# Cross-attention with a gated mix and an eight-expert feed-forward on one core: masks filled earlier, one h on ScalarE, two weight chunks loaded later

## The reference

```
h      = (x - mean(x)) / sqrt(var(x) + 1e-5)                 # layernorm over the 256 columns
normed = h * rsqrt(mean(h*h) + 1e-6) * norm_w
pool   = concat([normed, ctx], positions)                    # 256 keys
logits = (normed @ q_w.T) @ (pool @ k_w.T).T / 16            # causal for the first 128 keys
h_t    = softmax(logits) @ pool
alpha  = sigmoid(h @ gate_w.T + gate_b)
x2     = x + (1 - alpha) * h + alpha * h_t
xn     = layernorm(x2), as 2048 token rows
for each expert e of 8 (tok = top_idx[:, e], 512 rows):
    y   = gelu(xn[tok] @ W1[e] + b1[e]) @ W2[e] + b2[e]       # 256 -> 1024 -> 256, tanh gelu
    acc[tok] += y * combine_weights[tok, e]
out    = x2 + acc                                            # acc starts at zero
```

## Time and profile before

| | us |
|---|---|
| median of three runs | 276.34 (276.28 to 276.38) |
| profiled execution | 277.63 |
| its span, first to last instruction | 275.8 |
| TensorE busy | 265.7 (96% of the span) |
| VectorE / ScalarE / GpSimd busy | 219.0 / 188.2 / 155.9 |
| mean granted TensorE clock | 0.991 |
| chain that ended last | TensorE 83%, VectorE 6%, waiting for issue 4%, GpSimd 3%, ScalarE 2%, DMA 1% |

### The profile page before, as it was taken

One profiled execution on the slowest core, in us unless ns is written; L12 is line 12 of the kernel. 1 busy time (PEld: TensorE's weight loads), 2 busy tenths in 40 slices (PEclk: granted clock), 3 DMA queues, 4 the chain that ended last, 5 costly groups with the idle time before them and its releaser, 6 DMA issues.

```text
span 275.8 us, 5127 instructions
## 1 busy us (share of the span) xinstructions
PE 265.7 (96%) x1474; PEld 226.7 (82%) x1474; DVE 219.0 (79%) x554; ACT 188.2 (68%) x349; POOL 155.9 (57%) x153
## 2 busy tenths in 40 slices
PE   6999999999989999999999999999999999999992
PEld 2688899999866888888888888888888888888992
DVE  1788999898986499968878896796887889689452
ACT  2488898887575976685677587658657758763540
POOL 4283865655843956556446466655645646605515
PEclk9799999999999999999999999999999999999998
DMA  7993247568454956455565544546555461201211
GB/s 219 358 263 94 77 123 218 155 214 276 114 182 123 350 160 157 124 192 167 138 195 163 154 139 135 157 122 209 156 138 189 156 175 53 67 26 47 62 38 69
DMA packets 30292, 42.44 MB, mean 154 GB/s; under 512 B 5251, under 2 KB 24015, under 8 KB 30148
## 3 DMA queue, kind: packets, MB, share of 16 engines
q1 hardware_dynamic: 25392, 30.00, 34.4%
q0 software_dynamic: 4608, 12.24, 15.4%
q10 hardware_dynamic: 276, 0.00, 0.1%
HBM read 33.54 MB, written 9.24 MB: 155 GB/s over the span
## 4 chain that ended last, share of the span: by engine, by line
PE 83%; DVE 6%; issue 4%; POOL 3%; ACT 2%; DMA 1%; DVEq 0%; POOLq 0%; ACTq 0%
PE bank L1398 19%; PE bank L1185 13%; PE bank L1186 12%; PE bank L1187 12%; PE bank L1399 10%; PE bank L1229 4%; PE bank L1274 3%; PE bank L1326 2%; PE bank L1345 1%; PE bank L1349 1%; PE bank L1346 1%; DMA x_all<-in_x_dram 1%; PE bank L1181 1%; POOL out_dram L552 1%; PE bank L1258 1%
## 5 line engine op out<-in xcount | busy, mean ns | idle before, releaser
L742 ACT ACTIVATE keysT<-bank,biasT 128x512 f32<-128x512 f32 x63 | 43.7, 693 | 55.6 <-PE bank L1187 41.8
L552 POOL DMA_INDIRECT out_dram<-h,sidx x32 | 36.8, 1151 | 41.9 <-DVE h L1077 37.0
L543 POOL DMA_INDIRECT x_all<-out_dram,idx_all x32 | 35.4, 1106 | 23.9 <-DMA out_dram<-h,sidx 16.5
L1185 PE MATMUL bank<-x_hi,w_parts 128*128 128x512 f32 (+1 forms) x114 | 45.1, 396 | 0.0
L1186 PE MATMUL bank<-x_lo,w_parts 128*128 128x512 f32 (+1 forms) x114 | 44.4, 389 | 0.0
L1187 PE MATMUL bank<-x_hi,w_parts 128*128 128x512 f32 (+1 forms) x114 | 44.1, 387 | 0.0
L1102 DVE TENSOR_TENSOR g_lo<-keysT,g_hi 128x512 fp32r<-128x512 f32 x32 | 22.1, 690 | 24.9 <-ACT g_hi L743 23.4
L1398 PE MATMUL bank<-w_parts,g_hi 128*128 128x512 f32 x112 | 40.5, 396 | 0.0
L539 POOL DMA_INDIRECT x_all<-token_rows,idx_all x28 | 29.0, 1036 | 19.4 <-DVE factor L1126 7.7
L1107 DVE TENSOR_TENSOR w_parts<-w_raw,w_parts 128x512 fp32r<-128x512 f32 x56 | 38.9, 696 | 0.0
L748 ACT CAST w_parts<-w_raw 128x512 fp32r<-128x512 f32 x56 | 34.9, 623 | 0.0
(11 more groups left out here) (186 smaller groups left out, 685.9 us busy)
## 6 DMA issues: line engine op xcount, KB each, us to landing
w_raw<-in_L_ffn_W_dram SPq DMA_DIRECT2D x32, 512.0 KB
idx_rows<-in_L_ffn_top_idx_dram SPq DMA_DIRECT2D x8, 256.0 KB, 4.0
out_dram<-x SPq DMA_DIRECT2D x8, 256.0 KB, 3.0
hn_cnat<-in_ctx_dram SPq DMA_DIRECT2D x7, 256.0 KB, 2.7
token_rows<-xn SPq DMA_DIRECT2D x7, 256.0 KB, 2.2
hn_cnat<-in_L_ffn_b_dram SPq DMA_DIRECT2D x1, 1024.0 KB, 6.9
x_all<-in_x_dram SPq DMA_DIRECT2D x3, 256.0 KB, 4.4
x_all<-in_x_dram SPq DMA_DIRECT2D x1, 768.0 KB, 8.1
```

What stands on the lines that cost most here:

```text
L543: g.indirect_dma_start(accg[:, t, :], None, flat, list_of(e, t)).then_inc(acc_in[t], 16)
L552: g.indirect_dma_start(flat, idx(sidx[:, t:t + 1].bitcast(U32), 0), newrow[:, t, :], None, bounds_check=N - 1, oob_is_err=False).then_inc( ...
L742: a.activation(g32[:, f % NG, :], ps_up[f % 2][:, :], ACT.Gelu_apprx_tanh, bias=bias)
L1185: t_.matmul(dst, lhs_hi, rhs_hi, start=first, stop=False)
```

## The change

- Start: k_w is loaded by ScalarE's queue, ahead of norm_w, and not by SyncE's. norm_w and gate_b are loaded with one value per partition, and spread by four transposes of a broadcast column in place of the product with a row of ones. M's second half is made ahead of the first hn transposes, the context's transposes and copy ahead of the query. One more warm-up product. On VectorE both halves of M_lo come ahead of hnT_lo; the statistics of batch rows 6 to 9 are split and end behind pair 0's gate logits.
- Expert 0's chunks 2 and 3 are issued in rounds 0 and 1 of SyncE's loop over pairs, and expert 1's chunks 2 and 3 behind b2 after the loop. The last list part is loaded after the last rows' stores. ScalarE waits for chunk 2 in pairs 2 and 4, for chunk 3 in pair 6.
- Pairs 6 and 7: ScalarE makes h of pair 7, as a scaled and shifted identity. VectorE makes `stats2` and `aggr2` right behind the residual, and `shift` behind the gate logits. Piece 5 of expert 0's low weights goes from GpSimd to VectorE. GpSimd gathers tiles 0 and 1 in pair 7 ahead of rstd and tiles 2 and 3 behind it. ScalarE makes its weight piece earlier in pair 7 and later in pair 6.
- Passage: the products of late and early rows are put in another order; the first half of the last late_lo comes ahead of the last shift.
- Masks: `seen` is filled as 1024 float32 numbers whose bits are two bfloat16 ones, and masks are made before expert 1's gathers, when the last rows are ready.
- End: the last two up blocks come before the down products of blocks 4 to 7, which all go tile by tile; the waits before the last scatters stand in the scatters themselves.

The core of the diff (names of semaphores that follow from it, and repeated lines, are left out):

```diff
+    ONE_ONE = 1.0 + 0x3F80 / 2 ** 23
+        def stats_first(pair):
+            return isinstance(pair, int) and pair >= LAST - 1
...
@@ SyncE
-            load_weight(1, k_w, wts_in)
-            for c in range(NCH):
-                sp.dma_start(w_chunk_dst(c), w_chunk(0, c)).then_inc(w_in[c], 16)
+            for c in range(2):
+                load_chunk(0, c)
...
                 if r == LAST:
...
+                    sp.wait_ge(onehot_rdy, NB - EARLY)
+                    load_lists(IDX_PARTS - 1)
-                if r % 2 == 1:
+                if r < 2:
+                    load_chunk(0, 2 + r)
+                if r in (1, 3):
                     sp.wait_ge(wlo0_rdy, r + 1)
-                    sp.dma_start(w_chunk_dst(r // 2), w_chunk(1, r // 2)).then_inc(w_in[r // 2], 16)
+                    load_chunk(1, r // 2)
             sp.wait_ge(pv_mm, NPAIR)
             row_broadcast(b2_bc, b2.rearrange("e h -> (e h)")).then_inc(b2_in, 16)
+            for c in range(2, NCH):
+                sp.wait_ge(wlo0_rdy, 2 * c + 2)
+                load_chunk(1, c)
@@ GpSimd, attention
                 if is_last(p):
-                    gather_first_rows(range(1, NT))
+                    gather_first_rows(range(2))
...
-                    if not is_last(p):
+                    if not stats_first(p):
                         expert0_lo(p - 1)
                     rstd(p - 1, 1 - s)
-                if p == LAST - 1:
-                    gather_first_rows(range(1))
+                if is_last(p):
+                    gather_first_rows(range(2, NT))
@@ GpSimd, after the pairs
+            pool.wait_ge(pv_mm, NPAIR)
+            pool.wait_ge(last_xn[1], 1)
+            g.memset(seen_pairs, ONE_ONE).then_inc(consts, 1)
+            pool.wait_ge(consts, 4)
+            for t in range(NT):
+                g.affine_select(out=seen[:, t, :], ...).then_inc(seen_rdy, 1)
             for s in range(2):
                 pool.wait_ge(xn_out[s], ...)
                 pool.wait_ge(x2_out[s], ...)
             gather_rows(1, 1)
-            pool.wait_ge(pv_mm, NPAIR)
-            g.memset(seen, 1.0).then_inc(consts, 1)
...
@@ ScalarE
+            act.dma_start(wts[:, 1, :, :], k_w.rearrange("(k p) h -> p k h", p=P)).then_inc(wts_in, 16)
...
+            def last_h_rows():
+                act.wait_ge(hs_rdy, 5)
+                act.wait_ge(xh_rdy, LAST - 1)
+                act.wait_ge(diff_rdy, 2 * LAST - 2)
+                for b in range(2):
+                    a.activation(h[:, 1, b, :], x3[:, 2 * LAST + b, :], ACT.Identity, bias=last_h_shift[:, b:b + 1],
+                                 scale=pow_out[:, 0, 2 * LAST + b:2 * LAST + b + 1]).then_inc(h_rdy, 1)
...
+                if is_last_but_one(p):
+                    last_h_rows()
+                if is_last(p):
+                    expert0_hi(p)
...
-                    for c in range(NCH):
+                    for c in range(2):
                         act.wait_ge(w_in[c], 16)
+                elif not isinstance(p, int) and s == 0:
+                    act.wait_ge(w_in[2], 16)
+                if not is_last(p) and not is_last_but_one(p):
+                    expert0_hi(p)
@@ VectorE, attention
                     residual(p - 1, 1 - s, last_use)
+                    if stats_first(p):
+                        stats2(p - 1, 1 - s)
+                        aggr2(p - 1, 1 - s)
...
+                    if stats_first(p):
+                        shift(p - 1, 1 - s)
-                    if not is_last(p):
+                    if not stats_first(p):
                         h_rows(p + 1, 1 - s)
@@ VectorE, after the pairs (last_pair_low is the late_lo[2] of one row)
+            last_pair_low(0)
             last_pair_shift(1)
...
+            last_pair_low(1)
-            for piece in range(NPAIR - 2, NPAIR):
+            for piece in range(NPAIR - 3, NPAIR):
@@ TensorE, start
             M_rows(0)
+            M_rows(1)
             hn_transposes(0, 0)
-            M_rows(1)
-            t_.matmul(banks[7][:, :], ones_row[:, :], vec_rows[:, :], start=True, stop=True).then_inc(bc_mm, 1)
+            for n in range(2):
+                for k in range(KH):
+                    last = t_.transpose(banks[7][:, ...], norm_w_gate_bT[:, n, k:k + 1].broadcast_to([P, P]), ident[:, :])
@@ TensorE, last_downs and expert
-                    for f in range(NF - 3, NF):
+                    for f in range(NF - 4, NF):
-                    if not (is_last(e) and f == NF - 1):
+                    if not (is_last(e) and f >= NF - 2):
                         down(e, s, f - 2)
```

More of the change, by code:

```diff
@@ L147, in build_xattn_moe @@
             .rearrange("p (t c) -> p t c", t=NT)
+        seen_pairs = normed[:, :, :, :].rearrange("p s b h -> p (s b h)")
         cnat_last = x_all[:, NT * ROW:NT * ROW + 2 * H].rearrange("p (b h) -> p b h", b=2)
@@ L301, in each_pair, with is_last_but_one @@
             body(LAST, 1, 3)
+        def is_last_but_one(pair):
+            return isinstance(pair, int) and pair == LAST - 1
+        def stats_first(pair):
+            return isinstance(pair, int) and pair >= LAST - 1
         def has_second_next(pair):
@@ L949, in attention @@
                 if is_first(p):
+                    x_aggregates(6, 10)
+                    x_variances(6, 10)
                     h_rows(1, 1, False)
                     x_stats(10, NB, 4)
-                else:
+                elif not stats_first(p):
                     stats2(p - 1, 1 - s)
@@ L958, in attention @@
                 else:
-                    aggr2(p - 1, 1 - s)
-                    if not is_last(p):
+                    if stats_first(p):
+                        shift(p - 1, 1 - s)
+                    else:
+                        aggr2(p - 1, 1 - s)
+                    if not stats_first(p):
                         h_rows(p + 1, 1 - s)
@@ L971, in attention @@
                     dve.wait_ge(x_steps, steps[0])
-                elif not is_last(p):
+                elif not stats_first(p):
                     shift(p - 1, 1 - s)
@@ L1017, in _ @@
             last_pair_mixed(0)
-            shift(NPAIR - 2, 1 - last_s)
             last_pair_variance(0)
@@ L1030, in _ @@
                             ALU.mult, ALU.add).then_inc(last_xn[1], 1)
-            for b in range(2):
-                dve.wait_ge(late_hi_rdy, 3 + b)
-                dve.wait_ge(last_xn[b], 1)
-                v.tensor_tensor(late_lo[2][:, b, :], xn_last[:, b, :], late_hi[2][:, b, :].bitcast(F32),
-                                ALU.subtract).then_inc(late_lo_rdy, 1)
+            last_pair_low(1)
             def x_lo_part(e, s):
@@ L1250, in attention @@
                         .then_inc(setup_mm, 1)
-                    pe.wait_ge(log_rdy, 2 * NPAIR - 1)
-                    pe.wait_ge(late_hi_rdy, 1)
-                    for b in range(2):
-                        late_rows(0, b, late_hi, first=b == 0)
                 pe.wait_ge(exp_rdy, 2 * p + 2)
@@ L1264, in attention @@
                 if is_last(p):
-                    early_rows(range(1))
+                    pe.wait_ge(log_rdy, 2 * NPAIR - 1)
+                    pe.wait_ge(late_hi_rdy, 1)
+                    for b in range(2):
+                        late_rows(0, b, late_hi, first=b == 0)
                 pe.wait_ge(pT_ev, p + 1)
```

111 lines of the change are left out of this document (64 added, 47 removed).

## The result

The changed kernel took 280.57 us (median of four runs, 279.08 to 281.75) against 276.31 before: a ratio of 1.0151 (95% interval 1.0101 to 1.0201). The forecast was 273.8, faster. The profiled execution took 280.89, its span is 279.1.

A forecast was written before the change was run, and what follows sets the result against it. Nothing starves TensorE in the expert stage, so slack lies in the start, passage and end. Terms 1.6 - 0.7 + 1.0 + 0.65 = 2.55 us off the median 276.34 gave 273.8 us, range 272.0 to 276.0.

The forecast's parts named there:

- The weight chunks: Late loads of expert 0: ScalarE waits 1.4 us for chunk 2 in pair 2; cost 0.7 us, from 0 to 1.2.
- The start: Up to pair 2's logits: earlier query starts pair 0's logits at 12.35, gain 1.6 us at pair 2, from 0.3 to 2.6.
- Rival 1: Start: clock stays at half through the first query, costing 1.3 us, total 275.1; chance 0.17.
- The passage: Pairs 6 and 7 to the first x_hi, set by VectorE: gain 1.0 us, from 0.4 to 1.4.
- The masks: Masks ahead of expert 1's gathers end at 86.5 to 87.4 and cost nothing, with 1.3 us in hand.
- rival 3: Masks hold VectorE: three weight pieces each behind a select make g_lo(0) 2.3 us late, total 275.3; chance 0.07.
- rival 4: Last list load, moved behind the last rows, holds ScalarE before expert 0's second gelu: 4 us lost, 277.8; chance 0.06.
- The expert stage: Expert products on TensorE: nothing starves them and they stay in place, so the stage can only begin earlier.
- The end: Last up product before block 4's down products: first scatter 0.8 us earlier, gain 0.65, from 0.3 to 0.9.

The follow-up runs named there:

- e5: Kernel before, unchanged, profiled again in a single execution: 276.01 us.
- e1: Changed kernel with all four chunks of expert 0 loaded at the start again, as before: 275.79 us, ratio 0.9975 to before.
- e3: Changed kernel with chunk 2 loaded at the start and only chunk 3 late, in round 1: 277.44 us, ratio 1.0037 to before.
- e9: e1 with the new 8-byte tensor of ScalarE's h declared behind all others: 275.04 us, ratio 0.9944 to before.
- e12: e1 with a pad declared between the weights and x_hi: 276.25 us, ratio 0.9989 to before.
- e15: Kernel before with ten warm-up products, not nine: 276.21 us, ratio 0.9980 to before.
- e11: Changed kernel with one late chunk a round, ScalarE's wait for chunk 2 in pair 4 only, and the new 8-byte tensor declared last: 275.07 us, ratio 0.9948.
- e10: Kernel before with one unused 8-byte tensor declared at the place of the new one: 277.17 us, ratio 1.0029 to before.
- e8: e1 with the end of the kernel before: 276.58 us, ratio 0.9999 to before.
- e13: e11 with the last list loaded where it was before, ahead of the last store of x2: 274.65 us, ratio 0.9931 to before.
- e14: Kernel before with only chunks 2 and 3 of expert 0 loaded late, in rounds 0 and 1: 281.81 us, ratio 1.0190.
- e7: Kernel before, unchanged, profiled once more in a single execution: 277.74 us.

## Why the prediction was wrong

The profiled execution after against e5, an ordinary execution of before, by stretches of TensorE's timeline and chain:

| stretch | before (e5) | after | change | forecast |
|---|---|---|---|---|
| to the logits of pair 2 | 30.28 | 29.69 | -0.6 | -1.6 |
| to those of pair 4 | 15.44 | 17.15 | +1.7 | +0.7 |
| to those of pair 5 | 7.72 | 11.70 | +4.0 | 0 |
| to those of pair 7 | 14.84 | 14.84 | 0 | 0 |
| to the first product of expert 0 | 15.69 | 14.93 | -0.8 | -1.0 |
| to expert 1's transposes | 11.72 | 12.06 | +0.3 | 0 |
| to the last transposes | 135.89 | 136.55 | +0.7 | 0 |
| to the end of the span | 42.62 | 42.18 | -0.4 | -0.65 |
| span | 274.2 | 279.1 | +4.9 | -2.55 |

- **The weight chunks** are the step that failed: costed at 0.7, they took 4.8 us by e1, 5.7 in the profiled execution. The forecast followed chunk 2 to the wait of ScalarE, and there its mechanism was right and only the size off: the load left at 33.70, behind the list as foreseen, ScalarE stood 2.1 and not 1.4, and 1.5 to 1.7 of it reached TensorE. The term that was too small is the landing: the cast behind the wait starts at 39.55, some 5.8 us after the issue, against 5.0. (Halfway between 4.1 and 6.9 would have been 5.5; the sum took a third.) For chunk 3 it asked when the chunk is wanted ("in pair 6 only") and not what is queued behind it: in round 1 it goes out with expert 1's chunk 0, and the context of pair 5 comes next. That is 1.65 by itself (e3), 4.0 in the profiled execution, where the clock falls behind the wait.
- **The start** was near by its own steps (12.35, with two errors that cancel; at pair 2 a gain of 2.2 on the trace, forecast at 1.6) and wrong in the base. The forecast saw that the trace lay 1.3 above the median, and took the gain off the median all the same. But those 1.3 were the half clock at 8 to 11 us, which the change removes and an ordinary execution does not have: against e5 the start gains 0.6, and 0.0 to 0.5 with all chunks early (e9 30.26, e1 30.09, e12 29.74). Rival 1, the clock staying at half, did not come: the four spreading transposes take 0.62, near the 0.60 at full clock, and e15 shows that the tenth warm-up product alone is enough in the kernel before.
- **The passage** was right by the traces: 0.8 against 1.0, mix(6) at 0.69 as foreseen. No run undoes it alone.
- **The masks** cost nothing, as foreseen; rival 3 did not come. VectorE's three pieces took 2.12 us from 89.51 on, 0.71 each; only the first stood beside a select, the last, which ended at 89.88. By the rule of the Trainium skill that the forecast named (SBUF — State Buffer, Who interferes with whom) a piece could have been held for a whole select; this trace shows no such hold, in an overlap of 0.37 us that hardly tests it. Expert 0's first blocks are 0.3 longer all the same. In e11 the late list (rival 4's place, far from its price) holds 0.25 of this; in the profiled execution of the changed kernel ScalarE did not wait for the list, and what its 0.3 are is not settled.
- **The expert stage** was costed at nothing because none of its instructions change. Its tensors moved: 0.8 us (e9, e10), a loss that no row of the trace before shows.
- **The end** was right: 0.64 by the traces of e8 and e1. First scatter to last is 4.20, against 4.05 in the earlier trace rows, as the wider tiles let expect.

No rival named the failed step. With the three losses mended and the last list back in its place the terms left add up: e13's trace against e5 is 0.64 shorter to the logits of pair 2, 0.76 in the passage and 0.65 at the end, 0.3 longer in pairs 2 to 7 and 0.1 at expert 0, which makes the 1.6 between the spans (272.6 and 274.2).

## What to carry to other kernels

Before a load is moved, write down what comes next on its queue and who waits for that: the load's own due time is half the question. A trace that lies well above the median holds something that most runs don't, and a gain on that stretch must not be subtracted from the median. When a small tensor is added, compare the addresses of what the longest stage reads: a stage whose code is untouched can still change its speed.

## What the runs showed of the hardware

- Eight bytes declared ahead of the expert stage's operands made an expert 23.22 us long, not 23.11 (e10 against before, e1 against e9); eight more between the weights and x made it 23.28 (e12). By the declared sizes, rounded up to 32 bytes each, the operands move between multiples of 64 and odd multiples of 32.
- One more idle product at the start left no run of 12 above 276.46 us (e15), where 9 of 18 beside them took over 277. In traces the slow start is 1.3 to 1.8 us long (e14, e7 against e5).
- After TensorE had waited 2.2 us for a load, its granted clock was 0.95, 0.50 and 0.69 in the next three stretches of 2 us, and products that take 0.28 us took 0.41 (after); behind waits of 1.8 (e3) and 2.3 (e14) they took 0.28.
- The record of the granted clock can read 1.00 while four products take 1.91 us that take 1.03 in another execution.
